# A mixture-of-experts stage whose row scatters are chained: each waits until the one before it has landed

## What is computed

```python
scores = sigmoid(xf @ gate_w.T + lb_bias)            # xf: the 4096 normalised rows
topw, topi = top_k(scores, 2)                        # two experts for each row
topw = topw / (topw.sum(-1, keepdims=True) + 1e-08)
for e in range(8):
    m = topi == e
    sel = m.any(axis=-1)
    wmean = (topw * m).sum() / maximum(m.sum(), 1)
    y = _mlp(xf, expert_gate_w[e], expert_up_w[e], expert_down_w[e])
    out = out + where(sel[:, None], y * wmean, 0)
out = out + _mlp(x, shared_gate_w, shared_up_w, shared_down_w)
```

## Time and profile before

| | |
|---|---|
| Time of the kernel before, median of 3 runs | 2126.75 us |
| Lowest and highest of the 3 runs | 2122.39 and 2129.96 us |
| Span of the profiled execution, first to last instruction | 2196.9 us |
| Share of the span: PE busy, DVE, ACT, POOL | 87%, 70%, 56%, 19% |

### The profile page before, as it was taken

The page is one execution under the profiler, slowest core; times in us unless marked ns, Lnnn a source line. Parts: engine busy times, 40 slices in busy tenths (PEclk is TensorE's granted clock), DMA queues, the critical chain, the costliest instruction groups (busy, mean ns, idle before and its releaser), DMA issues. The chain is left out here.

```text
span 2196.9 us, 35579 instructions
## 1 busy us (share of the span) xinstructions
PE 1921.0 (87%) x12028; PEld 1004.6 (46%) x12028; DVE 1531.1 (70%) x3120; ACT 1233.3 (56%) x2476; POOL 426.0 (19%) x514
## 2 busy tenths in 40 slices
PE   6898895789999999999999999999999855558893
PEld 4665664434434444444444444444433234436673
DVE  6888884677787787787787787788789344232344
ACT  2311312157767777777777777777777732124441
POOL 1100102202103113112112112212210003240334
PEclk9999997589989999999999999999999976678997
DMA  7300002442521621621621621621610021123553
GB/s 239 122 0 0 0 1 77 80 76 76 94 61 63 108 61 57 114 61 54 117 61 51 120 61 50 120 61 41 130 31 2 1 76 46 53 94 121 163 184 100
DMA packets 82493, 166.14 MB, mean 76 GB/s; under 512 B 12176, under 2 KB 54544, under 8 KB 82192
## 3 DMA queue, kind: packets, MB, share of 16 engines
q1 hardware_dynamic: 76192, 147.35, 28.4%
q0 software_dynamic: 6144, 16.79, 2.4%
HBM read 95.72 MB, written 67.65 MB: 74 GB/s over the span
## 5 line engine op out<-in xcount | busy, mean ns | idle before, releaser
L1157 DVE TENSOR_REDUCE x_mx<-x_ps 128x1 f32<-128x512 f32 x1536 | 975.5, 684 | 221.3 <-PE x_ps L902 212.4
L1062 ACT ACTIVATE x_probs<-x_ps 128x512 f32<-128x512 f32 (+1 forms) x1664 | 894.3, 597 | 281.8 <-PE x_ps L966 275.9
L966 PE MATMUL x_ps<-x_qst,x_kst 50*128 50x512 f32 (+1 forms) x1664 | 595.7, 453 | 24.0 <-ACT x_probs L1062 21.8
L902 PE MATMUL x_ps<-x_kst,x_qst 48*128 48x512 f32 x1536 | 574.8, 462 | 17.6 <-DMA x_kst<-k_parts 11.0
L950 PE MATMUL x_ps<-x_probs,x_vst 128*17 128x512 f32 (+1 forms) x3328 | 446.7, 609 | 4.8 <-ACT x_ou L1045 4.8
L902 PEld LDWEIGHTS x_ps<-x_kst,x_qst 48*128 48x128 f32 x1536 | 240.3, 191 | 435.2 <-DVE x_mx L1157 288.8
L966 PEld LDWEIGHTS x_ps<-x_qst,x_kst 50*128 50x128 f32 (+1 forms) x1664 | 243.3, 183 | 116.3 <-ACT x_probs L1062 110.8
L1094 POOL TENSOR_TENSOR x_vst<-x_v_all,x_bv 128x768 f32<-128x768 f32 x64 | 66.5, 1069 | 379.5 <-ACT x_v_all L1020 300.8
L285 ACT ACTIVATE r_qwide<-r_qT,r_headmask 128x512 f32<-128x512 f32 x128 | 80.0, 709 | 105.0 <-DVE r_qT L435 105.0
L214 PE MATMUL r_ps<-r_qwide,r_kT 128*128 128x512 f32 x256 | 116.2, 602 | 10.0 <-DVE r_vz L441 10.0
L888 PE MATMUL x_ps<-x_ctxT,x_wk 128*128 128x256 f32 (+1 forms) x448 | 123.5, 402 | 0.0
(11 more groups left out here) (221 smaller groups left out, 2201.3 us busy)
## 6 DMA issues: line engine op xcount, KB each, us to landing
x_kst<-k_parts SPq DMA_DIRECT2D x192, 200.1 KB, 8.5
k_parts<-x_kp SPq DMA_DIRECT2D x16, 1601.0 KB, 5.9
x_ctxT<-in_ctxT SPq DMA_DIRECT2D x8, 1601.0 KB, 8.2
x_qst<-q_parts SPq DMA_DIRECT2D x192, 64.0 KB, 2.9
sorted_x<-s_zero SPq DMA_DIRECT2D x2, 4992.0 KB, 29.6
f_xt<-sorted_x SPq DMA_DIRECT2D x26, 384.0 KB
sorted_y<-f_yt SPq DMA_DIRECT2D x26, 384.0 KB
q_parts<-x_qp SPq DMA_DIRECT2D x8, 1024.0 KB, 4.2
```

Of the source, the lines that this page charges most:

```text
L902: m = pe.matmul(o, qst[mg][rows, pair, t * P:(t + 1) * P], kst[mg][rows, pair, i * 512:(i + 1) * 512], start=True, stop=True)
L966: pe.matmul(ps[0:w, n % S_BANKS, :], kst[g][rows, pair, c * P:c * P + w], qst[g][rows, pair, :], start=True, stop=True).then_inc(s_filled, 1)
L1062: nc.scalar.activation(probs[0:w, s % (2 * GH), :], ps[0:w, s % S_BANKS, :], ACT.Exp, scale=HD ** -0.5).then_inc(exp_done, 1)
L1157: nc.vector.tensor_reduce(out=mx[:, 2 * pair + half, t, i:i + 1], in_=o, axis=AX.X, op=ALU.max).then_inc(drained_v, 1)
```

## The change

One line is added ahead of the scatter: POOL waits until `scattered[h]` stands at 16 for each scatter of this half issued before it, that is until all of them have landed. `at_least` leaves out a wait for 0, so the first scatter of each half has no such wait. The other 62 have one. Nothing else is changed; no instruction is added, removed or moved on any engine.

```diff
@@ -1648,6 +1648,7 @@
                 for t in range(h * HTILES, (h + 1) * HTILES):
                     for k in range(TOPK):
                         at = index[:, t * TOPK + k:t * TOPK + k + 1]
+                        at_least(pool, scattered[h], 16 * ((t - h * HTILES) * TOPK + k))
                         nc.gpsimd.indirect_dma_start(rows.x[h], bass.IndirectOffsetOnAxis(at, 0), xn[:, t, :],
                                                      None).then_inc(scattered[h], 16)
```

## The result

| | before | after |
|---|---|---|
| Median of the timed runs | 2124.57 us (2120.06 to 2129.96, 4 runs) | 2209.01 us (2196.51 to 2214.08, 4 runs) |
| Span of the recorded execution | 2196.9 us | 2201.2 us |
| Time of that execution | not given | 2204.54 us |

The changed kernel takes 1.0358 times as long, 95% interval 1.0301 to 1.0414: 76 us more, 64 to 88. The medians are 84 us apart. The forecast was 2187 us, 60 more than before. So the sign was right and the cost too small. The time is inside the range (2122 to 2210) by 1 us, and 1 us above the 2208 that the sum gave with its dearest terms. The two recorded spans are only 4.3 us apart (the prediction had 3.7, the other way): the execution recorded of before was slower than its timed runs.

A forecast was written before the change was run, and what follows sets the result against it. PE is busy 9 tenths or more through most of the span; its feed-forward halts were taken as recording-only. Chaining moves tile 39 from 1976.3 to 2036.6 us: 2126.75 + 60.3 = 2187 us, range 2122 to 2210.

The forecast's parts named there:

- the freeze: Feed-forward stage: PE halts beside back-to-back scatters and gathers; 64 us and 6.36 us, taken as only in the recorded execution.
- no other part can give up 70 us: Outside the feed-forward stage: cross attention is full of PE work, retention's 300 us window has 46 us idle.
- the tie to the pace: Feed-forward scatters and gathers: PE halts when they run back to back, not with gathers 1.63 us or more apart.
- Rival 1: Feed-forward scatters: PE's halt is real and chaining cures it; 2123 us, 2102 to 2144; chance 0.21.
- Rival 2: Feed-forward scatters: chain dearer, 3.1 us a step with 25 us of hold-up; +106 us, 2233 us; chance 0.06.
- Rival 3: Feed-forward scatters: rows land before POOL is ready for the next scatter, so no wait; 2126.75 us; chance 0.03.
- undisturbed base: Feed-forward stage of the kernel before without PE's halts: tile 39 would come at 1976.3 us, not 2040.32.
- step: Each chained scatter on POOL: 2.60 us, between 2.42 and 2.70, in place of 1.27.
- load: SP's first load behind a half's last scatter: 2.5 us until the tile can start.
- cold clock: PE after its 27 us wait ahead of tile 0: clock fallen to 0.50, slow first steps, 2 us more.
- hold-up: Second half's chained scatters: some 11 pairs of 384 KB loads and stores delay them 0 to 25 us, 10 taken.
- the gathers were covered as claimed: First half's gathers behind the scatters on POOL: start about 2038, first wanted by DVE at 2048; covered by some 5 us.

The follow-up runs named there:

- experiment 1: The kernel before, unchanged, recorded and timed once more: 2121.57 us, ratio 0.9974 against before.
- 4: The kernel before with POOL clearing a small buffer twice behind each scatter, no wait for a landing: 2127.57 us, ratio 1.0001 against before.
- 6: The kernel before with each scatter waiting for the last but one, so two can be under way: 2128.52 us, ratio 1.0027 against before.
- Experiment 7: The changed kernel with loads 3 to 12 and stores 0 to 12 cut to 16 of 128 partitions: 2181.96 us, ratio 1.0272 against before.
- the second comparison: The changed kernel once more, no edit, against the kernel before on the same chip: 2217.59 us, ratio 1.0439.

## Why the prediction was right, and where it was too small

**Whether the freeze is in the timed runs.** This was the step that decided the sign, and it was right: it set two numbers of the same kernel against each other, a span of 2196.9 us and a median of 2126.75. Of the 46 executions of before that the later comparisons timed or recorded, the longest span is 2151.3 us. Span and time lie 1.8 to 3.0 us apart in all of them, and 3.3 in the recorded execution of after. The gap of 70 us between span and median was thus no overhead but another execution. The Trainium skill (Runtime: NRT & Kernel Launch, section "The ~15µs preamble/postamble breakdown") gives the profile's total as some 6.2 us longer than the reported time. Here the span, from first to last instruction, is the shorter one; whether that total is the same thing as this span, no run here shows.

That the trace made up for the gap to 0.4 us (70.5 against 70.15) was luck. From the first scatter to the end the recording of before took 348.6 us and the four others 270.4 to 271.6. So 77 to 78 us went in its stage: 63 to 65 of them ahead of tile 39 and 12 to 14 behind it, where the prediction had counted 6.36. The rest hid in two places. That recording began the stage at 1842.4 us, some 5 to 6 us sooner than a run of 2126.75 us would (an estimate: in the four others time less the first scatter's start is 278.3 to 279.6 us). And a span is some 2 us shorter than the time it stands for. The prediction's reason that no other part can give up 70 us also skipped 340 to 480 us, where PE is busy 102.72 of 140 us at a clock of 0.65. Experiment 1 has 104.42 us at 0.64 there, so next to nothing went in that stretch.

What was too strong is the tie to the pace. The prediction read the freeze as something that back-to-back scatters bring in a recorded execution, and experiment 1 expected it again; four other recordings of before have back-to-back scatters and no freeze. What brought it is not settled, and no run here could bring it back.

**Rival 1,** a real freeze that chaining cures, is refuted by experiment 1 (back-to-back scatters, PE 17.06 of 20 us busy) and by 4 and 6, which space or limit the scatters and gain nothing. **Rival 2,** a dearer chain, was right about the second half, where loads and stores run beside the chain and 32 steps average 3.2 us; but the first half's average 2.7, with no such transfers, and the time stayed below its 2233. **Rival 3,** a wait that is no wait, falls by POOL's 123.7 us of waits.

**The terms of the sum.** All in us from the first scatter's start:

| step | predicted | measured | difference |
|---|---|---|---|
| tile 0 (31 steps, landing, load) | 85.5 | 90.4 | +4.9 |
| tile 0 to second half's first scatter | 13.25 | 11.1 | -2.1 |
| second half's scatters until landed | 93.0 | 101.2 | +8.2 |
| last load to tile 39 | 2.5 | 3.6 | +1.1 |
| tile 39 | 194.2 | 206.3 | +12.1 |
| tile 39 in the undisturbed base | 133.9 | 134.6 | +0.7 |
| cost at tile 39 | 60.3 | 71.7 | +11.4 |

- The **step** was taken as 2.60 us between 2.42 and 2.70. It is 2.67: the landing and POOL's waking add up in full (2.40 + 0.27). Taking the upper end would have been right, since SP's load showed the landing without POOL's waking in it. That is 2.2 us a half, and a few single steps beside shared rounds took longer (3.9 us at 1857.87), for a reason that no run here shows. The Trainium skill (DMA: Bandwidth & Descriptors, section "Anatomy of one DMA — SWDGE (gpsimd) path") gave 2.30 us as an estimate; the chain shows 2.40, and the wake has to be added.
- The **load** was taken as 2.5 us; from the landing to the tile it is 3.3 and 3.6.
- The **cold clock** after the wait was put at 2 us and cost nothing here: 11.1 us from tile 0 to the second half's first scatter, against 11.25 in the earlier trace rows and 11.4 in experiment 1.
- The **hold-up** by loads and stores was the mis-sized term with the widest bounds, 0 to 25 us, of which 10 were taken. 32 steps of 2.67 us would be 85.4; the measured 101.2 leave 16. Experiment 7 confirms the cause: with thin transfers 13 of them go.
- Behind tile 39 nothing is added: from there to the end it is 136.7 us in after and 136.3 in experiment 1, so the gathers were covered as claimed.

**What stays open.** The recordings put the cost at 72.1 us (343.0 against 270.9 from the first scatter to the end), and the second recording of after at 73.1. The timed medians say 84, and 92 in the second comparison; the intervals of the ratios come to 64 to 88 and 77 to 109 us. The rest isn't in the stage as recorded. The two recorded executions of after differ by 14.8 us in time and by 15.3 in where the stage begins. Time less the first scatter's start is 278.3 to 279.6 us in the four undisturbed recordings of before, and 352.3 and 351.7 in the two of after: 72 to 74 us, whatever came ahead of the stage.

For executions that were timed and not recorded only the mean clock is there to go by. In the 46 executions of before, the time falls by 1.7 us for each 0.001 of mean granted clock (0.926 to 0.947), with 2.7 us of scatter around that line. The two waits are some 70 us at half clock, which alone would bring an average execution of before (0.939) to about 0.925, an estimate: (0.939 x 2126 + 0.5 x 72) / 2198. Two runs of after are there (0.924 and 0.925), and take 2204.54 and 2196.51 us, 79 and 71 above 2125.8, the median of the 46. The other six have 0.913 to 0.920, and take 2213 to 2223. That fits an excess of the kind that before's own runs show among themselves, the lower clock ahead of the stage, but only one of the six was recorded. Whether the changed kernel meets it more often (six of eight runs; 16 of the 46 of before are at 2134 us or more) or by chance, these runs don't tell. This open part is also what decides whether the time lies in the predicted range: the second comparison's median, 2217.59 us, lies above it, so that the first one lies inside is partly luck.

## What to carry to other kernels

Compare the recorded execution's span with the timed runs before a cost is read from it: a stall that only the recording has can turn the sign, and a second recording is the test. A chain of DMAs costs landing plus the issuer's waking at each link, here 2.67 us in place of 1.27, and the loads and stores of 384 KB lengthened it only while they ran beside it; two in flight gave the speed back with almost the same waits, the second half with nothing to spare. What such a chain costs is its lengthening less the cover at each consumer, here 12 us ahead of tile 0 (loads could start at 42.7 us in experiment 1 and take 3.3; the tile came at 57.6), and each half pays for itself.

## What the runs showed of the hardware beyond that

- One of five recordings of the same kernel held stalls of 77 to 78 us in all, in which ACT waited up to 25.34 us for PE's results; neither of the two of the chained kernel did.
- A chained scatter of 128 rows took 2.40 us to be seen as landed while nothing else moved (1915 to 1939 us of after), and up to 4.85 us beside loads and stores of 384 KB. With two in flight a pair took 2.67 us.
- The end of cross attention ran at a granted clock of 1.00 in one execution and of 0.50 in others; the same 16 matmuls took 3.69 us and 5.31, and the stage's first scatter started between 1840.4 and 1867.6 us over all recordings.
